# Softmax sums from a column of ones in the values, weighing in quarters of the array, and weights split on GpSimd

## The reference

```python
x_freq = _ln_c(_dct_rearrange(feat), n1_w, n1_b)
x_spac = _ln_c(feat, n2_w, n2_b)
# _win_attn, twice: q from one of them, k and v from the other; windows of 64 tokens, 8 heads of 32
attn = jnp.einsum('bhnd,bhmd->bhnm', q, k)
attn = jax.nn.softmax(attn + bias[None], axis=-1)
out = jnp.einsum('bhnm,bhmd->bhnd', attn, v).transpose(0, 2, 1, 3).reshape(Bw, N, C)
out = out @ wo.T + bo
# then: concatenation, a 1x1 convolution, a 3x3 convolution, statistics over the batch
```

## Time and profile before

| | |
|---|---|
| median of 3 runs | 839.13 us (835.7 to 839.85) |
| the profiled execution, own time | 843.31 us |
| its span in the profile | 841.5 us |
| PE busy | 649.7 us, 77% |
| DVE busy | 578.2 us, 69% |
| ACT busy | 345.7 us, 41% |
| POOL busy | 80.5 us, 10% |

### The profile page before, as it was taken

How to read it: one execution, slowest core, us unless ns; L and a number is a source line. 1 busy time by engine, 2 the same in 40 slices (tenths; PEclk the granted TensorE clock), 3 DMA queues, 4 the chain that set the end, 5 groups by cost and what they waited for, 6 DMA issues and landing times.

```text
span 841.5 us, 19916 instructions
## 1 busy us (share of the span) xinstructions
PE 649.7 (77%) x8560; PEld 547.0 (65%) x8560; DVE 578.2 (69%) x1316; ACT 345.7 (41%) x750; POOL 80.5 (10%) x101
## 2 busy tenths in 40 slices
PE   4547697988979797767985467879788887887867
PEld 3436586877768686655873355767666676776755
DVE  2375778787786868316745365978897787888764
ACT  3243333433434524117851263445454445454520
POOL 0000000000000000004771010101010101010000
PEclk8667899999999899986996576898998899989797
DMA  5020301011010000001200212020303030303000
GB/s 210 32 70 2 112 15 48 7 43 36 13 36 2 2 2 2 1 26 51 76 1 26 38 37 28 26 39 13 64 15 63 1 76 2 76 2 88 2 14 13
DMA packets 28264, 29.68 MB, mean 35 GB/s; under 512 B 1936, under 2 KB 22544, under 8 KB 28048
## 3 DMA queue, kind: packets, MB, share of 16 engines
q1 hardware_dynamic: 28176, 28.41, 13.3%
HBM read 22.11 MB, written 6.29 MB: 34 GB/s over the span
## 4 chain that ended last, share of the span: by engine, by line
PE 18%; DVE 18%; DMA 7%; ACT 6%; issue 3%; SPq 3%; POOL 2%; DVEq 0%; POOLq 0%; ACTq 0%
PE ps L205 11%; DMA ks<-rope_scratch 5%; DVE mx L1267 4%; DVE e2l L1279 3%; PE ps L997 3%; SPq L875 3%; ACT prob L1115 2%; ACT e2h L1123 2%; DMA rope_scratch<-rl 2%; PE ps L891 1%; DVE acc L1351 1%; DVE rl L1254 1%; PE ps L984 1%; DVE st L1190 1%; DVE cl_moe L1208 1%
## 5 line engine op out<-in xcount | busy, mean ns | idle before, releaser
L1115 ACT ACTIVATE prob<-ps,nmx 128x128 f32<-128x128 f32 (+1 forms) x256 | 83.1, 436 | 131.4 <-DVE nmx L1273 131.4
L205 PE MATMUL ps<-secondh,ch_moe 128*128 128x256 f16 (+1 forms) x320 | 88.1, 282 | 22.2 <-DVE cl_moe L1208 14.2
L205 PE MATMUL ps<-secondh,cl_moe 128*128 128x256 f16 (+1 forms) x320 | 87.8, 281 | 0.0
L205 PE MATMUL ps<-secondl,ch_moe 128*128 128x256 f16 (+1 forms) x320 | 87.6, 281 | 0.0
L205 PE MATMUL ps<-yh,wconvh 128*128 128x256 f16 x288 | 81.2, 282 | 3.1 <-DVE yl L744 3.1
L1279 DVE TENSOR_TENSOR e2l<-ps,e2h 128x512 f16<-128x512 f32 x96 | 61.6, 686 | 30.4 <-ACT e2h L1123 29.6
L205 PE MATMUL ps<-yh,wconvl 128*128 128x256 f16 x288 | 81.2, 282 | 0.0
L205 PE MATMUL ps<-yl,wconvh 128*128 128x256 f16 x288 | 80.9, 281 | 0.0
L1267 DVE TENSOR_REDUCE mx<-ps 128x2 f32<-128x512 f32 (+1 forms) x96 | 60.4, 682 | 19.9 <-PE ps L987 19.9
L997 PE MATMUL ps<-cst,prob 128*128 128x128 f32 x384 | 65.1, 329 | 6.9 <-ACT prob L1115 6.2
L984 PE MATMUL ps<-ks,qs 80*128 80x128 f16 (+1 forms) x256 | 40.9, 271 | 29.9 <-DMA ks<-rope_scratch 24.6
(11 more groups left out here) (202 smaller groups left out, 1940.1 us busy)
## 6 DMA issues: line engine op xcount, KB each, us to landing
weights_stage<-in_second SPq DMA_DIRECT2D x6, 684.0 KB, 4.4
qs<-rope_scratch SPq DMA_DIRECT2D x48, 64.0 KB
ks<-rope_scratch SPq DMA_DIRECT2D x48, 64.0 KB
weights_stage<-in_wconv SPq DMA_DIRECT2D x6, 384.0 KB, 3.6
xw<-in_xw SPq DMA_DIRECT2D x8, 256.0 KB, 2.8
xc<-in_xc SPq DMA_DIRECT2D x8, 256.0 KB, 2.7
rope_scratch<-rh SPq DMA_DIRECT2D x8, 256.0 KB, 2.2
rope_scratch<-rl SPq DMA_DIRECT2D x8, 256.0 KB, 2.2
```

The source lines that it names most:

```text
L205: last = nc.tensor.matmul(out_ap, lhs[x], rhs[w], start=done == 0, stop=done == n - 1)
L1115: last = nc.scalar.activation(prob[:, c0:c0 + keys], psum[c % 2][:, c0:c0 + keys], ACT.Exp, scale=SOFTMAX_SCALE, bias=nmx[:, m:m + 1])
```

## The change

The values get a 33rd column for each head and window, ones in the high part and zeros in the low part, set once by GpSimd. Weighing then yields the sum of the exponentials beside the 32 weighted values. The sum over the rows and its semaphore leave VectorE; in weigh it takes four reciprocals from PSUM, and four products over all 128 partitions write `o`. The matmuls of weigh are cut by window: 64 by 64 tiles of the array, four of them for the two heads and the two windows, with 33 moving columns, 192 matmuls an image.

normalise becomes scalar_tensor_tensor, with the inverse deviation broadcast as a tensor. For the weights of the later stage (images 2 to 7) ScalarE scales the staged piece in place in a second activation, and GpSimd subtracts the high part; VectorE keeps the convolution's weights. GpSimd's new step `weights` stands in its own queue behind `dct`.

```diff
-        vh, vl = pair("vh", [P, 2, TILES, 4, 2 * HD], f16), pair("vl", [P, 2, TILES, 4, 2 * HD], f16)
+        vh, vl = pair("vh", [P, 2, TILES, 4, 2, HD1], f16), pair("vl", [P, 2, TILES, 4, 2, HD1], f16)
...
                 pe.wait_ge(el_done[p], i * 4 + 4)
+                pe.wait_ge(columns_set, 4)
...
                                 for hh in range(2):
                                     rows = slice(64 * hh, 64 * hh + 64)
-                                    c0 = (at * 2 + t) * BANK + r * P
-                                    d0 = (t * 4 + r) * 2 * HD
-                                    last = nc.tensor.matmul(bank(p, at * 2 + hh)[:, d0:d0 + 2 * HD],
-                                                            e[rows, c0:c0 + P], v[p][rows, at, t, r],
-                                                            start=n == 0, stop=n == 2)
+                                    d0 = (t * 4 + r) * HD1
+                                    for w in range(2):
+                                        c0 = (at * 2 + t) * BANK + r * P + w * WTOK
+                                        last = nc.tensor.matmul(
+                                            bank(p, at * 2 + hh)[64 * w:64 * w + 64, d0:d0 + HD1],
+                                            e[rows, c0:c0 + WTOK], v[p][rows, at, t, r, w],
+                                            start=n == 0, stop=n == 2)
...
                     nc.scalar.activation(high, stage[slot][:, 0:width], ACT.Copy,
                                          scale=S).then_inc(weights_high, 1)
+                    if i:
+                        nc.scalar.activation(stage[slot][:, 0:width], stage[slot][:, 0:width], ACT.Copy,
+                                             scale=S).then_inc(weights_scaled, 1)
...
+            for p in range(2):
+                nc.gpsimd.memset(vh[p][:, :, :, :, :, HD], 1.0).then_inc(columns_set, 1)
+                nc.gpsimd.memset(vl[p][:, :, :, :, :, HD], 0.0).then_inc(columns_set, 1)
...
+            def weights(p, i):
+
+                for n, slot, _, width, _, high, low in weight_chunks(p, i) if i else ():
+                    pool.wait_ge(weights_scaled, n - CONV_CHUNKS + 1)
+                    nc.gpsimd.tensor_tensor(low, stage[slot][:, 0:width], high, ALU.subtract).then_inc(weights_split, 1)
...
-                        last = nc.vector.tensor_scalar(xn[:, s, t, :], tokens(p, s, t), mv[:, n, 0:1],
-                                                       rstd[:, n:n + 1], ALU.subtract, ALU.mult)
+                        last = nc.vector.scalar_tensor_tensor(xn[:, s, t, :], tokens(p, s, t), mv[:, n, 0:1],
+                                                              rstd[:, n:n + 1].to_broadcast([P, C]),
+                                                              ALU.subtract, ALU.mult)
...
-                rows = prob[:].rearrange("p (g m) -> p g m", m=WTOK)
-                dve.wait_ge(exp_done[p], i * 2 + 2)
-                nc.vector.tensor_reduce(sums[:], rows, op=ALU.add, axis=AX).then_inc(sum_done[p], 1)
-                dve.wait_ge(sum_done[p], i + 1)
-                nc.vector.reciprocal(rs[:], sums[:]).then_inc(recip_done[p], 1)
...
                     for hh in range(2):
-                        pv = bank(p, at * 2 + hh).rearrange("p (t r w d) -> p t r w d", t=2, r=4, w=2)
-                        for w in range(2):
-                            rows = slice(64 * w, 64 * w + 64)
-                            nc.vector.tensor_tensor(
...
+                        nc.vector.reciprocal(inverse[:, at, hh], pv[hh][:, :, :, HD]).then_inc(recip_done[p], 1)
+                    for hh in range(2):
+                        dve.wait_ge(recip_done[p], i * 4 + at * 2 + hh + 1)
+                        nc.vector.tensor_tensor(
+                            o[:, at, :, hh * P:(hh + 1) * P].rearrange("p t (r d) -> p t r d", r=4),
+                            pv[hh][:, :, :, 0:HD],
+                            inverse[:, at, hh].unsqueeze(3).to_broadcast([P, TILES, 4, HD]),
+                            ALU.mult).then_inc(o_done[p], 1)
...
-                for n, slot, _, width, _, high, low in weight_chunks(p, i):
+                for n, slot, _, width, _, high, low in weight_chunks(p, i) if i == 0 else ():
                     dve.wait_ge(weights_high, n + 1)
```

More of the change, by code:

```diff
@@ L25 @@
 ITERS = B // 2
+HD1 = HD + 1
 VEC = {}
@@ L340, in windows @@
         eh, el = one("eh", [P, 4 * BANK], f16), one("el", [P, 4 * BANK], f16)
-        sums, rs = one("sums", [P, 32]), one("rs", [P, 32])
+        rs = one("rs", [P, 32])
         o = one("o", [P, 2, TILES, C])
@@ L358, in windows @@
                               "conv_done", "z_done"))
-        sum_done = sems("sum_done")
-        pads_set, half_set = sem("pads_set"), sem("half_set")
+        pads_set, half_set, columns_set = sem("pads_set"), sem("half_set"), sem("columns_set")
         weights_loaded = sems("weights_loaded")
-        weights_high, weights_split = sem("weights_high"), sem("weights_split")
+        weights_high, weights_scaled, weights_split = sem("weights_high"), sem("weights_scaled"), sem("weights_split")
         def weight_chunks(p, i):
@@ L382, in by_window @@
         def by_window(v, p, at, t):
-            return v[p][:, at, t].rearrange("p r (w d) -> p w r d", w=2)
+            return v[p][:, at, t, :, :, 0:HD].rearrange("p r w d -> p w r d")
         def image(im, oh, wi):
@@ L496, in weigh @@
                                     rows = slice(64 * hh, 64 * hh + 64)
-                                    c0 = (at * 2 + t) * BANK + r * P
-                                    d0 = (t * 4 + r) * 2 * HD
-                                    last = nc.tensor.matmul(bank(p, at * 2 + hh)[:, d0:d0 + 2 * HD],
-                                                            e[rows, c0:c0 + P], v[p][rows, at, t, r],
-                                                            start=n == 0, stop=n == 2)
+                                    d0 = (t * 4 + r) * HD1
[5 more added lines that the diff above has]
+                                            start=n == 0, stop=n == 2)
                     last.then_inc(pv_done[p], 1)
             def out_channels(p, i):
-                pe.wait_ge(o_done[p], i * 8 + 8)
+                pe.wait_ge(o_done[p], i * 4 + 4)
                 for h in range(HALVES):
@@ L601, in weights @@
             def weights(p, i):
-                for _, slot, before, width, _, high, _ in weight_chunks(p, i):
+                for n, slot, before, width, _, high, _ in weight_chunks(p, i):
                     act.wait_ge(weights_loaded[slot], before * 16 + 16)
@@ L626, in dct @@
                 nc.gpsimd.tensor_tensor(rstd[:], rstd[:], half[:], ALU.pow).then_inc(rstd_done[p], 1)
-            pipeline(pool, WINDOW_ORDERS, WINDOW_AHEAD, WINDOW_LOOP, {"dct": dct})
+            def weights(p, i):
+                for n, slot, _, width, _, high, low in weight_chunks(p, i) if i else ():
+                    pool.wait_ge(weights_scaled, n - CONV_CHUNKS + 1)
+                    nc.gpsimd.tensor_tensor(low, stage[slot][:, 0:width], high, ALU.subtract).then_inc(weights_split, 1)
+            pipeline(pool, WINDOW_ORDERS, WINDOW_AHEAD, WINDOW_LOOP, {"dct": dct, "weights": weights})
         @block.vector
@@ L713, in weigh @@
             def weigh(p, i):
-                dve.wait_ge(recip_done[p], i + 1)
-                inverse = rs[:].rearrange("p (a t r h) -> p a t r h", a=2, t=2, r=4)
+                inverse = rs[:].rearrange("p (a h t r) -> p a h t r", a=2, h=2, t=TILES)
                 for at in range(2):
                     dve.wait_ge(pv_done[p], i * 2 + at + 1)
+                    pv = [bank(p, at * 2 + hh)[:, 0:8 * HD1].rearrange("p (t r d) -> p t r d", t=TILES, r=4)
+                          for hh in range(2)]
                     for hh in range(2):
-                        pv = bank(p, at * 2 + hh).rearrange("p (t r w d) -> p t r w d", t=2, r=4, w=2)
-                        for w in range(2):
-                            rows = slice(64 * w, 64 * w + 64)
-                            nc.vector.tensor_tensor(
[L724 to L727, removed]
+                        nc.vector.reciprocal(inverse[:, at, hh], pv[hh][:, :, :, HD]).then_inc(recip_done[p], 1)
[6 more added lines that the diff above has]
+                            ALU.mult).then_inc(o_done[p], 1)
             def out_channels(p, i):
```

## The result

The changed kernel takes 860.12 us (median of 4 runs, 854.4 to 861.59) against 839.49 us (4 runs, 835.7 to 841.08) for the kernel before on the same chip: a ratio of 1.023, interval 1.0163 to 1.0296. It is slower by some 20.6 us. The profiled execution took 860.28 us (span 858.5), against 843.31 us (span 841.5) before.

A forecast was written before the change was run, and what follows sets the result against it. TensorE was taken to bound conv to scores, VectorE the rest of an image. Stops 13.3, weigh 1.0, weights and scores 4.3, clock 3, less 1.8, gave +19.8 us: 863 profiled, 859 median, range 842 to 871.

The forecast's parts named there:

- The stops: TensorE in or behind weigh, images 1 to 7: idle until the next program block arrives, 1.9 us each, 13.3 together.
- (a): Rival: no stops in weigh, as blocks come sooner or the pace outlasts the fetch; +3 us, 842 us; chance 0.08.
- (b): Rival: no stops, weigh bound by its 33 columns, 0.8 us a pass; -4.8 us, 834 us; chance 0.10.
- (c): Rival: slow weight loads in weigh without stops, 1.5 us more a pass; +12.5 us, 852 us; chance 0.07.
- (d): Rival: stops in every weigh, low clock behind most; +29 us, 868 us; chance 0.75 together with the main forecast.
- Weigh itself: TensorE's weigh, 96 matmuls becoming 192 smaller ones: +0.15 us a pass, +1.0 us over seven images.
- Weights' part and the scores: Weights' low part on GpSimd delays ocl 0.63 us; scores stop in three steady images, formerly one: +4.3 us together.
- The clock: TensorE's granted clock drops behind stops: +3 us taken, bounds -3 and +12.
- nine new stops: New stops forecast for TensorE; the low clock behind half of them would cost 7 us.
- the drop that the prediction names: TensorE's clock drops in the kernel before, at 289 us and after, which may fall elsewhere after the change.
- The first xn: First image's attention, without the sums on VectorE: xn 1.8 us earlier, gained once; bounds 0 and 2.6.
- the carrying over: Terms summed against the profiled execution, 4.2 us above the median, then applied to the median: 863 profiled, 859 median.

The follow-up runs named there:

- E3: Changed kernel with 40 dummy matmuls ahead of the first image on TensorE; 862.95 us, ratio 1.0251.
- E4: Changed kernel with weigh cut into two halves of 96 pairs, values and queries between them; 847.09 us, ratio 1.0053.
- E10: E8 with one more wait: SyncE's load of the later weights waits for normalise of the image before; 843.33 us, ratio 1.0028.
- E8: E4 with weights and normalise as before, step weights between to_channels and conv 1, last pass's weigh halves each behind a conv half; 848.94 us, ratio 1.0125.
- E2: Kernel before with only ScalarE's second activation, GpSimd's subtraction and scalar_tensor_tensor in normalise; 847.07 us, ratio 1.0057.
- E6: E2 with the step weights moved to between to_channels and conv 1; 839.36 us, ratio 0.9994.
- E7: Kernel before with step weights moved between to_channels and conv 1, and el ahead of the sums on VectorE; 841.47 us, ratio 0.9937.
- E9: E7 with one more wait: SyncE's load of the later weights waits for normalise of the image before; 837.11 us, ratio 0.996.

## Why the prediction held

**The stops.** Predicted: seven in or behind weigh, after pairs 197, 135, 200, 138, 203, 141, 193, of 1.5 to 2.4 us, 13.3 together. Measured: seven, after pairs 197, 136, 201, 140, 205, 144 and 195, idle for 1.50 to 2.17 us, together 12.25. The count drifts by half a pair an image because it has one more instruction for the new wait, while both traces have 102 event instructions. The time lost is more than the idle time: values took 3.55, 3.88 and 4.06 us instead of 1.67 in images 1, 3 and 5, weigh 3.68, 3.48 and 3.49 instead of 1.78 in images 2, 4 and 6, and in image 7 conv goes on 1.98 us late. That is 13.7 us, 0.1 of low clock in image 2 left out. The step that carried the sum was to read q8's packets as blocks of 256 and count the program. E3 and E4 show it: moved by 40 pairs, the stops move; cut in two, they go. Rivals (a) and (b), no stops, and (c), slow loads without stops, are refuted by the same rows, and (d) too, since the low clock came behind two of the seven stops only (below).

The Trainium skill (Runtime: NRT & Kernel Launch, Instruction fetch mechanics) has the blocks of 256 instructions, and that the next one is fetched while one runs: this trace agrees, by 73 packets of 16.4 KB and stops 256 x n instructions apart. It also says that this is mostly hidden, as dispatch is slower than the fills. Here it is not, at 8.3 ns a pair.

**Weigh itself.** 1.78 us a pass where 1.57 + 0.15 was taken: +0.21, seven times, 1.5 us for 1.0. The scores' row was the right neighbour. The Trainium skill (TensorE: Matmul & The Clock Gate, weight-path modes) would have 2.6 us by my estimate from its slow load; 192 loads of 64 columns in 1.68 us of PEld say otherwise for tiles that share the array.

**Weights' part and the scores.** ocl comes 0.65 us later (predicted 0.63). Scores stop in images 0, 2, 4, 6, as counted. From the start of the scores to that of turn 10.03 us pass in an undisturbed image of before, and 11.20 in its image 4. In after it is 10.68 in images 3, 5 and 7, and 11.31, 11.28 and 11.39 in images 2, 4 and 6, where the scores stop. Over the six images that is 4.7 us more, for 4.3 predicted. Before had a stop more than I saw: in image 5's pass project starts at 246.41, 0.9 us after ocl ended at 245.51, at the grid's instruction 6593. The wait is put down to ocl, which had long been done. This stop cost nothing, since turn still starts 10.03 us after the scores.

**The clock.** This is the term that was mis-sized. Predicted +3 us, chosen below the 7 us that the low clock behind half of nine new stops would cost. The low clock came, but mostly elsewhere. The 24 matmuls of project ran slow in nearly every image of after; the stretch over them in image 2:

```profile
132.22:136.90 4.68, 4.68 (x32) 3.59 (x27) 4.54 (x6) 0.00 (x0) 0.28 (x1) 0.64 0.46 153
```

That is beside VectorE's bias and maximum and costs nothing. Behind weigh it came in two of the seven images. Behind the stop of image 2, PE over 5 us at a granted 0.66:

```profile
160.00:165.00 5.00, 5.00 (x97) 4.56 (x85) 1.75 (x6) 0.86 (x3) 0.00 (x0) 0.66 0.03 7
```

There values and queries took 8.44 us instead of 7.02: with weigh's end 1.5 us lost. In image 7 the half of conv behind weigh took 9.81 us instead of 6.30, 1.98 by the stop and 1.5 by the clock (0.83). But the kernel before lost time by the clock too, in turn and the first half of conv. In image 3 (full clock), behind the scores' stop of image 4, and in image 6, at the drop that the prediction names:

```profile
175.07:183.72 8.65, 8.44 (x72) 7.12 (x73) 6.44 (x19) 3.72 (x9) 1.21 (x2) 1.00 0.08 10
213.84:223.58 9.74, 9.74 (x72) 8.62 (x73) 7.49 (x21) 3.84 (x9) 1.20 (x2) 0.82 0.11 29
290.10:301.04 10.94, 10.94 (x72) 9.41 (x73) 8.70 (x23) 3.95 (x9) 1.21 (x2) 0.72 0.01 1
```

In after the same work took 8.65 us in images 1 to 6, and in image 7 9.74 us in both kernels. So before lost 1.1 and 2.3 us that after did not, and the clock's term, by these two profiled executions, is 1.5 + 1.5 - 1.1 - 2.3 = -0.4 us, and not +3: the low clock moved and did not add. The prediction allowed for that in its bounds (-3 to +12) but not in its value.

**The rest.** The first xn came at 63.84 instead of 65.41: 1.6 us for 1.8 predicted. A pair of normalise took 0.87 us (predicted between the two forms' 0.73 and 0.96) and is hidden. GpSimd's subtraction took 2.77 us (estimated 2.8). The reciprocals of 8 columns took 0.27 us for two. The 40 us of DVE's busy time that went (578.2 to 538.8) gave nothing beyond the first image.

**The sum.** In the first stage: 13.7 + 1.5 + 4.7 - 0.4, less 1.35 by which the second image's turn comes earlier (80.01 us after the first memset, where it was 81.36), is 18.1 for the measured 18.0 and a predicted 19.8. The clock was put 3.4 us too high. That the sum came within 2 us is in part luck, for the other terms were 1.7 us too low together: 0.4 for the stops, 0.5 for weigh itself, 0.4 for the weights and scores, and 0.4 or 0.5 for a gain in the first image that was smaller than predicted. The second stage was 1.0 us shorter, within its scatter. For the profile 863 was predicted and 860.28 came, for the median 859 and 860.12. The profile of before lay 4.2 us above its median and that of after at it, so the carrying over was right only within that scatter.

## What to carry to other kernels

Count TensorE's instructions as well as its columns: where a run of small matmuls at 8.3 ns a pair (192 here) is longer than a block of the program (128 pairs), the next block can be late by 1.5 to 2.2 us, and cutting a matmul in two to save VectorE's work can make such a run. Break the run with slow matmuls (E4 gave back 1.8% of the kernel), and keep large loads away from it (E10 against E8: 4.9 us of the first stage). Work taken from one engine gains nothing where its next instruction waits for an engine that the change loads (E2); moving the step off that wait can be worth more than changing the engine (E6 against E2: 7.4 us of the first stage).

## What the runs showed of the hardware beyond that

A data load beside such a row of small matmuls makes a stop where there was none, or lengthens it: the same instruction idles for 1.36 us with the load (E7, DMA share 0.79 and 0.98 in the two microseconds ahead of the stop) and 0.32 us without (E9, 0.07 or less). But the stops of the changed kernel need no load. The stretch of DMA from 112 to 120 us of the changed kernel, in 40 slices of 0.2 us, has one packet, of the program, ahead of the stop of image 1:

```profile
DMA  0000000000000000000000000300000000000000
```

It is seen at 117.0 us; the block before it was entered 69 pairs behind 115.70, at about 116.3; the stop ends at 119.43. From the packet to the resumption 2.4 us pass with the queues otherwise idle, so most of the 3.1 us is not the transfer (16.4 KB; the packet took 1.0 us, 0.8% of 16 engines' 8 us) but what stands around it. What that is no run here shows.
